# A layernorm, attention and spiking-FFN kernel: blocks 6 and 7 scaled by GpSimd and transposed by VectorE, and a lead of ten steps for the score maxima

## The chip, the cores and the metric

The kernel runs on one core of a Trainium2 chip. The metric is the device time of one launch, in microseconds (us); 3 runs of the kernel before gave a median of 1691.6 us (1691.52 to 1691.74). A core has TensorE (PE, matmuls), VectorE (DVE), ScalarE (ACT), GpSimd (POOL), and SyncE (SP), which here only issues DMAs. Each engine works through its own instructions in order, and they wait for one another by semaphores. Matmul results land in PSUM, which GpSimd does not touch in this kernel.

## The reference, cut to what matters

```python
xn = layernorm(x)                                  # x: 2 x 2048 x 256, float32, no affine part
q, k, v = split(xn @ w_qkv)                        # 16 heads of 16
q, k = irfft(rfft(q) * mask), irfft(rfft(k) * mask)   # mask = sigmoid(mask_logits), per head dim
attn = softmax(q @ k.T / sqrt(16)) @ v             # over 2048 keys, 2 batches x 16 heads
h = square(relu(xn @ W_fc.T)); y = h @ W_proj.T    # 1024 hidden
mem = 0                                            # then five times:
mem = 0.9 * mem + y - (mem > 1);  spk = mem > 1
out = x + attn @ w_out + b_out + mean(spk)
```

## The kernel before, in words

**The prologue** (0 to 111.5 us of the profiled execution) takes the 4096 tokens in eight blocks of 512 (`t` = 0 to 7). A block is normalised on VectorE: `block_stats` (four `bn_stats` and `bn_aggr`), `block_rstd` (a chain of small operations with one square root on ScalarE), and `block_scale` (four `tensor_scalar` of 128x256, subtract and multiply, with the mean and the reciprocal deviation as scalars per partition). The result has to be turned, because TensorE contracts over partitions. Two ways exist. Blocks in `TURNED` (1 to 5) are transposed in 32x32 squares by VectorE (`turn_block`, one instruction of 128x1024), and sixteen pieces of 32x256 are then moved to their place in `xnT`: ScalarE moves 8 (`MOVES` = 0, 2, 3, 3 behind the four `take_high` of the block before), GpSimd 8. Blocks 0, 6 and 7 are turned by eight 128x128 transposes on TensorE into PSUM (line 616), and ScalarE copies them out (`take_transposed`, line 506).

For each block TensorE then computes q and k (`project_qk`, line 659, four pieces `w` of 128x512) and v (`project_v`, line 672, eight matmuls of 128x256). The float32 matmuls are recorded as two instructions each. ScalarE rounds a piece of q or k to its high part (`take_high`, line 526), VectorE subtracts for the low part (`low_part`, line 1046), and both go to DRAM and come back as the operands `qst` and `kst` of the scores, with high and low parts stacked.

**The maxima.** Softmax needs the row maxima of the scores before the scores are made, because the shift by the maximum is added inside TensorE (line 724). So the scores are computed twice: first for the maxima, then transposed for the exponentials. A head's 2048x2048 scores have 32 units of maxima (128 queries x 1024 keys each) and 32 steps of scores. In the main loop the maxima run `LEAD` = 8 steps ahead. The first 24 units of the first head lie in the prologue: `FIRST_MAX` = 48 matmuls of 128x512 (`first_max`, TensorE line 645, VectorE line 1012), one behind every matmul of blocks 5, 6 and 7. Two halves of a PSUM buffer `mx` alternate, so that the first_max n+2 on TensorE waits until VectorE has reduced n.

**The main loop** (112.8 to 1658 us) has 16 pairs of steps for each of 32 heads (`pair`): in a pair TensorE makes four maxima matmuls (line 711), scores and shifts for two steps (lines 718 and 724), the products with V for two earlier steps (line 735), and a share of the FFN (lines 841 and 846). ScalarE takes the exponentials (line 562) and copies half a unit for VectorE (line 568); VectorE reduces the maxima (lines 1017 to 1036); GpSimd squares and runs the five spiking steps. Twice in a head `split_shift` turns 8 maxima per partition into the shift rows (VectorE lines 1058 to 1073), and SP stores them with eight DMAs (line 329). TensorE waits for these at steps 0 and 16 (`shift_in`). From step `ALONE` (8 steps into the last head) on there are no maxima left, and the pairs are shorter. The end (line 928) projects the attention output and VectorE adds the rest.

The order of every engine is written out by hand. Around the change it is set on VectorE by the loop over `t` and `w` after `normalise(1)`: in block 4 the three stages of block 6 stand behind the pieces `w` = 0, 1, 2, and the whole of block 7 behind piece 3. ScalarE waits in the same place with `deviation(7)`, and behind it stand a table load, `take_v(4)` and the first `take_high` of block 5:

```python
for w in range(QB):
    if t > 4:
        for n in range(2):
            first_max(TB * (t - 5) + 2 * w + n)
    low_part(t, w)
    if t == 4 and w < 3:
        (block_stats, block_rstd, block_scale)[w](6)
if t == 4:
    normalise(7)
```

Of the kernel before, what the change touches and what calls it, by code (L numbers as in the profile page):

```python
# [34 lines left out]
LEAD = 8  # L35
# [8 lines left out]
TURNED = range(1, 6)  # L44
MOVES = (0, 2, 3, 3)
POOL_MOVES = 16 - sum(MOVES)
USES = 3
# [22 lines left out]
def build(nc, x, wqk, wv, wout, bout, logits, wfc, wproj, dft, eye, out):  # L70
    with ExitStack() as ctx:
# [131 lines left out]
        ln_done = sem("ln_done")  # L203
        tr_done = sem("tr_done")
# [203 lines left out]
        def _(pool):  # L408
# [19 lines left out]

            pool.wait_ge(preset, PRESETS)
            for t in TURNED:  # L430
                pool.wait_ge(turned, t)
                for n, (dst, src) in enumerate(list(moves(t))[16 - POOL_MOVES:]):
                    if t > 1 or n:
                        pool.wait_ge(moved_pool, POOL_MOVES * (t - 1) + n)
                    pool.tensor_copy(dst, src).then_inc(moved_pool, 1)
            pool.wait_ge(moved_pool, POOL_MOVES * len(TURNED))

# [173 lines left out]
        def _(pe):  # L611
# [23 lines left out]
            def first_max(n):  # L635

                (tile, chunk), c = first_part(n), n % 2
                pe.wait_ge(mx_taken, n + 1)
                if n < 2:
                    pe.wait_ge(lo_done, QB * 4 + QK_BANKS + n + 1 + QK_BANKS)  # L640
                if n in (0, TB):
                    pe.wait_ge(keys_in[0][n // TB], KEYS)
                if n in (0, 2 * TB):
                    pe.wait_ge(queries_in[0][n // (2 * TB)], QUERIES)
                pe.matmul(mx[:, c, :], qst[0][:, tile * P:(tile + 1) * P], kst[0][:, chunk * BLK:(chunk + 1) * BLK],  # L645
                          start=True, stop=True).then_inc(mx_ready, 1)
# [289 lines left out]
        def _(dve):  # L936
            LN_LINKS = 7

            def block_stats(t):

                base, p = LN_LINKS * t, t % 2
# [8 lines left out]
                dve.wait_ge(ln_step, base + 1)  # L950
                dve.memset(carrier[:, 0:1], 0.0)
# [6 lines left out]
            def block_rstd(t):  # L958
                base = LN_LINKS * t
# [9 lines left out]
                dve.tensor_tensor(rstd[:, 4, :], rstd[:, 3, :], rstd[:, 2, :], ALU.mult).then_inc(ln_step, 1)  # L969
# [39 lines left out]
            def first_max(n):  # L1009
                tile, chunk = first_part(n)  # L1010
                dve.wait_ge(mx_ready, n + 1)
                dve.tensor_reduce(pmax[:, tile, chunk:chunk + 1], mx[:, n % 2, :], AX, ALU.max).then_inc(mx_taken, 1)
# [69 lines left out]
            for t in range(NB):  # L1082
# [4 lines left out]
                for w in range(QB):  # L1087
                    if t > 4:
                        for n in range(2):
                            first_max(TB * (t - 5) + 2 * w + n)  # L1090
                    low_part(t, w)
                    if t == 4 and w < 3:
                        (block_stats, block_rstd, block_scale)[w](6)
                if t < 4:
                    normalise(t + 2)
                if t == 4:
                    normalise(7)
# [42 lines left out]
            halve(1, pmax[:, TB // 2:TB, 0:2], FIRST_MAX)  # L1140
# [5 lines left out]
            def beside_maxima(h, b, s, last):  # L1146
# [6 lines left out]
                if s == LEAD + 2:  # L1153
                    for link in range(4):
                        split_shift(link, 2 * i + 1, 1, FIRST_MAX + g - 2)
# [8 lines left out]
                if s == LEAD + TB + 2 and not last:  # L1164
                    for link in range(4):
                        split_shift(link, 2 * i + 2, 0, FIRST_MAX + g - 2)
# [7 lines left out]
            def head(h, b, last=False):  # L1174
                for s in range(FIRST, STEPS + FIRST, 2):
# [11 lines left out]
                    if last and s == LEAD + TB:  # L1187
                        for t in END_LATE:
                            end_bias_of(t)
                    if last and LEAD + TB < s <= LEAD + TB + 12:  # L1190
                        end_base_of((s - LEAD - TB) // 2 - 1)
# [67 lines left out]
```

## Time and profile before

| | |
|---|---|
| median of 3 runs | 1691.6 us (1691.52 to 1691.74) |
| the profiled execution itself | 1691.07 us |
| its span, first to last instruction | 1689.3 us |
| busy: PE / DVE / ACT / POOL | 1681.4 / 1494.2 / 1330.1 / 719.7 us |
| granted TensorE clock | 1.0 of full speed |

Busy time alone does not show which engine is the bottleneck. What the end depends on is read from the chain of waits, which follows the last instruction back through whatever released each step. Idle times in square brackets in a timeline stand for the time just before a row and its releaser. The profiled execution is 1.8 us longer than its span.

### The profile page before, as it was taken

The numbers are of one execution on the slowest core, as the hardware profiler recorded it, in microseconds if no ns is written. First come the engines' busy times: TensorE is split into PE (matmuls) and PEld (weight loads), VectorE is DVE, ScalarE is ACT, GpSimd is POOL, SyncE is SP. The second block draws the span as 40 slices with busy tenths as digits, with TensorE's granted clock in tenths as the row PEclk, the third lists the DMA queues.
The fourth block names the chain that finished last, engine by engine and source line by source line (L and its number), as shares of the span: only waits on it lengthen the run. The fifth ranks groups of instructions, "written<-read, shape, count | busy, mean of one in ns | idle before, by whom it ended". The sixth has DMA issues, their size and how long they took to land.

```text
span 1689.3 us, 44435 instructions
## 1 busy us (share of the span) xinstructions
PE 1681.4 (100%) x17842; PEld 1145.9 (68%) x17842; DVE 1494.2 (88%) x2375; ACT 1330.1 (79%) x1718; POOL 719.7 (43%) x979
## 2 busy tenths in 40 slices
PE   9999999999999999999999999999999999999999
PEld 6566666666666666666666666666666666666667
DVE  6889999998999999989998999999989998999884
ACT  5548888888888888888888888888888888888872
POOL 3103334555433345554333455543335554333455
PEclk9999999999999999999999999999999999999999
DMA  6851122112211221122112211221122112211133
GB/s 216 294 161 47 33 54 55 51 33 55 55 50 34 55 55 43 41 55 55 43 41 55 56 37 47 55 55 36 48 55 56 31 53 55 55 30 54 43 105 103
DMA packets 95406, 108.02 MB, mean 64 GB/s; under 512 B 56032, under 2 KB 70240, under 8 KB 95200
## 3 DMA queue, kind: packets, MB, share of 16 engines
q1 hardware_dynamic: 91744, 101.97, 21.2%
q10 hardware_dynamic: 3456, 3.21, 0.6%
q8 instruction: 141, 2.31, 0.6%
q14 instruction: 65, 0.53, 0.1%
HBM read 78.91 MB, written 20.97 MB: 59 GB/s over the span
## 4 chain that ended last, share of the span: by engine, by line
PE 98%; DVE 1%; ACT 0%; issue 0%; ACTq 0%; POOL 0%; POOLq 0%
PE banks L735 31%; PE ring L711 22%; PE ring L718 14%; PE ring L724 14%; PE banks L841 7%; PE banks L846 3%; PE banks L659 2%; PE ring L928 2%; PE ring L672 1%; PE ring L645 1%; PE ring L659 1%; PE ring L686 0%; DVE stats L947 0%; DVE attnT L979 0%; ACT xnT L513 0%
## 5 line engine op out<-in xcount | busy, mean ns | idle before, releaser
L562 ACT ACTIVATE probs<-ring 128x1024 f32<-128x1024 f32 x1024 | 1002.1, 1026 | 6.5 <-PE ring L724 6.2
L711 PE MATMUL ring<-kst,qst 64*128 64x512 f32 x2000 | 674.7, 417 | 0.3 <-ACT probs L562 0.3
L735 PE MATMUL banks<-probs,vst 128*32 128x256 f32 x8192 | 548.2, 385 | 0.1
L1036 DVE TENSOR_REDUCE pmax<-ring 128x2 f32<-128x1024 f32 x407 | 497.7, 1223 | 12.7 <-PE ring L711 0.5
L568 ACT ACTIVATE half_sb<-ring 128x512 f32<-128x512 f32 x500 | 299.2, 598 | 261.4 <-PE ring L711 254.1
L718 PE MATMUL ring<-qst,kst 64*128 64x512 f32 x2048 | 493.0, 425 | 0.1
L711 PEld LDWEIGHTS ring<-kst,qst 64*128 64x128 f32 x2000 | 328.3, 184 | 208.3 <-issue 204.6
L1017 DVE TENSOR_REDUCE pmax<-ring 128x1 f32<-128x512 f32 x500 | 345.4, 691 | 88.7 <-PE ring L711 85.1
L724 PE MATMUL ring<-shift_rows,ones 64*128 64x512 f32 x2048 | 422.9, 390 | 0.0
L1023 DVE TENSOR_REDUCE pmax<-half_sb 128x1 f32<-128x512 f32 x500 | 335.5, 671 | 37.0 <-ACT half_sb L568 33.1
L735 PEld LDWEIGHTS banks<-probs,vst 128*32 128x32 f32 x8192 | 213.7, 109 | 209.7 <-issue 91.0
L841 PE MATMUL banks<-xnT,wfc_sb 64*128 64x128 f32 x2024 | 331.7, 284 | 0.1
L464 POOL TENSOR_TENSOR lif<-lif 128x256 f32<-128x256 f32 x32 | 19.7, 614 | 729.6 <-ACT y_sb L586 729.6
L846 PE MATMUL banks<-wproj_sb,hid_sb 64*128 64x256 f32 x1024 | 329.0, 401 | 0.0
L841 PEld LDWEIGHTS banks<-xnT,wfc_sb 64*128 64x128 f32 x2024 | 280.6, 186 | 19.6 <-PE ring L711 0.4
L718 PEld LDWEIGHTS ring<-qst,kst 64*128 64x128 f32 x2048 | 233.4, 185 | 26.5 <-ACT probs L562 3.6
L724 PEld LDWEIGHTS ring<-shift_rows,ones 64*128 64x128 f32 x2048 | 214.8, 185 | 17.2
L846 PEld LDWEIGHTS banks<-wproj_sb,hid_sb 64*128 64x128 f32 x1024 | 169.6, 184 | 10.9
L474 POOL TENSOR_SCALAR lif<-lif 128x256 f32<-128x256 f32 x128 | 110.1, 860 | 10.8
L475 POOL TENSOR_SCALAR lif<-lif 128x256 f32<-128x256 f32 x128 | 110.6, 864 | 8.0
L473 POOL TENSOR_TENSOR lif<-lif 128x256 f32<-128x256 f32 x128 | 95.1, 743 | 10.0
L471 POOL TENSOR_TENSOR lif<-lif 128x256 f32<-128x256 f32 x128 | 94.3, 737 | 10.0
(96 smaller groups left out, 1050.9 us busy)
## 6 DMA issues: line engine op xcount, KB each, us to landing
kst<-qk_scratch SPq DMA_DIRECT2D x256, 128.0 KB, 3.0
qst<-qk_scratch SPq DMA_DIRECT2D x256, 128.0 KB, 2.9
qk_scratch<-attnT SPq DMA_DIRECT2D x32, 256.0 KB, 3.0
shift_rows<-shiftT SPq DMA_DIRECT2D x512, 2.0 KB
qk_scratch<-probs SPq DMA_DIRECT2D x16, 256.0 KB, 3.0
attnT<-o_turned SPq DMA_DIRECT2D x256, 16.0 KB, 1.9
xnT<-x SPq DMA_DIRECT2D x8, 512.0 KB, 5.6
out<-xnT SPq DMA_DIRECT2D x7, 512.0 KB, 2.9
```

Of the source, the lines that this page charges most:

```text
L475: pool.tensor_scalar(decayed, mem, BETA, None, ALU.mult).then_inc(lif_step, 1)
L562: act.activation(probs[:, s % PS, :], score_slot(g), ACT.Exp, scale=SCALE).then_inc(exp_done, 1)
L568: act.activation(half_sb[:], unit_slot(2 * p)[:, BLK:2 * BLK], ACT.Copy).then_inc(half_taken, 1)
L711: return pe.matmul(unit_slot(g)[:, c * BLK:(c + 1) * BLK], qst[b][rows, tile * P:(tile + 1) * P], kst[b][rows, key:key + BLK], start=True, ...
L718: pe.matmul(score_slot(g)[:, c * BLK:(c + 1) * BLK], kst[b][rows_of(side), kt * P:(kt + 1) * P], qst[b][rows_of(side), q:q + BLK], start=T ...
L724: mm = pe.matmul(score_slot(g)[:, c * BLK:(c + 1) * BLK], ones[rows_of(side), :], shift_rows[rows_of(side), q:q + BLK], start=False, stop= ...
L735: mm = pe.matmul(po[32 * j:32 * (j + 1), half * D:(half + 1) * D], vst[b][:, kt, :], quarters[:, j], start=(kt == 0), stop=(kt == TB - 1))
L841: return pe.matmul(misc[:, (f % 4) * P:(f % 4 + 1) * P], wfc_sb[rows_of(side), c, f * P:(f + 1) * P], xnT[rows_of(side), c, tile * P:(tile ...
L846: return pe.matmul(misc[:, 0:D], hid_sb[rows_of(side), f, :], wproj_sb[rows_of(side), f, :], start=(f == 0 and side == 1), stop=(f == FC - ...
L1017: dve.tensor_reduce(pmax[:, tile, 2 * part:2 * part + 1], unit_slot(g)[:, 0:BLK], AX, ALU.max).then_inc(mx_taken, 1)
L1023: dve.tensor_reduce(pmax[:, tile, 2 * part + 1:2 * part + 2], half_sb[:], AX, ALU.max).then_inc(half_max, 1)
L1036: dve.tensor_reduce(pmax[:, tile, 2 * part:2 * part + 2], unit_slot(g).rearrange("p (c e) -> p c e", c=2), AX, ALU.max).then_inc(mx_taken, 1)
```

## The change

Three things change. GpSimd scales blocks 6 and 7 (`scale_block`), behind its moves of blocks 5 and 6; VectorE transposes them like blocks 1 to 5 (`TURNED` = 1 to 7), block 6 between the low parts of block 4 and the statistics of block 7, and block 7 inside block 5. GpSimd moves ten of the sixteen pieces and ScalarE six. And `LEAD` is 10: the first 44 instead of 48 first_max stay in the prologue, and the maxima in the last head go on for one pair more. The positions of `split_shift` in a head (steps 10 and 26) stay; `turn_output` goes from steps 12 and 28 to 14 and 30. In the code:

```diff
-LEAD = 8
+LEAD = 10
-TURNED = range(1, 6)
-MOVES = (0, 2, 3, 3)
+TURNED = range(1, 8)
+MOVES = (0, 2, 2, 2)
 POOL_MOVES = 16 - sum(MOVES)
+AFTER_MOVES = {6: 5, 7: 6}
...
+            def scale_block(t):
+                p = t % 2
+                pool.wait_ge(rstd_ready, t - NB + 3)
+                pool.wait_ge(turned, t - 2)
+                pool.wait_ge(moved_pool, POOL_MOVES * AFTER_MOVES[t])
+                for k in range(KT):
+                    last = pool.tensor_scalar(x_norm[:, p, k, :], x_in[:, p, k, :], meanvar[:, k, 0:1],
+                                              rstd[:, 4, k:k + 1], ALU.subtract, ALU.mult)
+                last.then_inc(ln_done, 1)
...
+                for n in (NB - 2, NB - 1):
+                    if AFTER_MOVES[n] == t:
+                        scale_block(n)
...
             def first_max(n):
+                if n >= FIRST_MAX:
+                    return
...
                 dve.wait_ge(ln_step, base + 1)
+                if t == NB - 1:
+                    dve.wait_ge(ln_done, NB - 1)
...
-                dve.tensor_tensor(rstd[:, 4, :], rstd[:, 3, :], rstd[:, 2, :], ALU.mult).then_inc(ln_step, 1)
+                last = dve.tensor_tensor(rstd[:, 4, :], rstd[:, 3, :], rstd[:, 2, :], ALU.mult)
+                last.then_inc(rstd_ready if t >= NB - 2 else ln_step, 1)
...
-                    if t == 4 and w < 3:
-                        (block_stats, block_rstd, block_scale)[w](6)
+                    if t == 4 and w < 2:
+                        (block_stats, block_rstd)[w](6)
+                    if t == 5 and w == 2:
+                        turn_block(7)
...
                 if t == 4:
-                    normalise(7)
+                    turn_block(6)
+                    block_stats(7)
+                    block_rstd(7)
...
-                if s == LEAD + 2:
+                if s == LEAD:
                     for link in range(4):
-                        split_shift(link, 2 * i + 1, 1, FIRST_MAX + g - 2)
+                        split_shift(link, 2 * i + 1, 1, FIRST_MAX + g)
...
-                if s == LEAD + TB + 2 and not last:
+                if s == LEAD + TB and not last:
                     for link in range(4):
-                        split_shift(link, 2 * i + 2, 0, FIRST_MAX + g - 2)
+                        split_shift(link, 2 * i + 2, 0, FIRST_MAX + g)
```

Where the instructions go, on VectorE first, from the last low parts of block 4 (`relu_sb`, `hid_sb`) to the third piece of block 5 in the kernel before. `probs<-attnT` would be a `turn_block`; `attnT<-attnT,meanvar,rstd` is a `block_scale`; `pmax<-ring` are first_max:

```order
L1046 TENSOR_TENSOR relu_sb<-ring,relu_sb 128x512
L979 TENSOR_SCALAR attnT<-attnT,meanvar,rstd 128x256 x4
L1046 TENSOR_TENSOR hid_sb<-ring,hid_sb 128x512
L947 BN_STATS stats<-attnT 128x6 x4
...
L969 TENSOR_TENSOR rstd<-rstd 128x4
L979 TENSOR_SCALAR attnT<-attnT,meanvar,rstd 128x256 x4
L1012 TENSOR_REDUCE pmax<-ring 128x1 x2
L1046 TENSOR_TENSOR attnT<-banks,attnT 128x512
```

The same place on VectorE now, as far as the transpose of block 7:

```order
L1072 TENSOR_TENSOR relu_sb<-ring,relu_sb 128x512
L1072 TENSOR_TENSOR hid_sb<-ring,hid_sb 128x512
L1013 STREAM_TRANSPOSE probs<-attnT 128x1024
L968 BN_STATS stats<-attnT 128x6 x4
...
L992 TENSOR_TENSOR rstd<-rstd 128x4
L1038 TENSOR_REDUCE pmax<-ring 128x1 x2
...
L1072 TENSOR_TENSOR attnT<-banks,attnT 128x512
L1013 STREAM_TRANSPOSE probs<-attnT 128x1024
L1038 TENSOR_REDUCE pmax<-ring 128x1 x2
```

Both `block_scale` are gone, and two transposes have come; the first stands ahead of the statistics of block 7. GpSimd before, from the last memset of the start to the first instructions of the main loop (`ISA` is the configuration instruction that the trace calls MODIFY_POOL_CONFIG):

```order
L419 MEMSET shift_rows 128x2048
L435 COPY xnT<-probs 32x4x2x32 x40
L440 COPY vst<-v_all 128x16x16
L452 ISA
L452 TENSOR_TENSOR hid_sb<-relu_sb 128x512
```

GpSimd now, the same stretch:

```order
L421 MEMSET shift_rows 128x2048
L447 COPY xnT<-probs 32x4x2x32 x50
L437 ISA
L437 TENSOR_SCALAR attnT<-attnT,meanvar,rstd 128x256 x4
L447 COPY xnT<-probs 32x4x2x32 x10
L437 TENSOR_SCALAR attnT<-attnT,meanvar,rstd 128x256 x4
L447 COPY xnT<-probs 32x4x2x32 x10
L455 COPY vst<-v_all 128x16x16
L467 TENSOR_TENSOR hid_sb<-relu_sb 128x512
```

The configuration instruction now stands between the moves of block 5 and the first scaling; the second scaling stands behind the ten moves of block 6.

## Rows read from the trace of the kernel before

**Rows 1.** The page's chain that ended last, shares by engine.
```profile
PE 98%; DVE 1%; ACT 0%; issue 0%; ACTq 0%; POOL 0%; POOLq 0%
```

**Rows 2.** Chain of waits, block 4: start us, length us, what.
```profile
51.45 0.69 DVE attnT L1046
...
56.77 1.25 DVE probs L989
...
64.71 1.31 DVE stats L947 x4
...
67.93 1.38 DVE attnT L979 x4
```

**Rows 3.** Timelines, blocks 0 to 5: start us, us, engine, line, operation [idle before].
```profile
22.95 3.70 PE L659 MATMUL banks<-xnT,counts 128*128 128x512 f32 x8 [0.31 <-ACT xnT L513]
...
58.08 3.63 POOL L435 COPY xnT<-probs 32x256 f32<-32x256 f32 x8 [6.48 <-DVE probs L989]
...
64.03 0.69 DVE L1046 TENSOR_TENSOR hid_sb<-ring,hid_sb 128x512 fp32r<-128x512 f32 x1
...
66.91 1.28 ACT L556 ACT_TABLE_LOAD   x1
...
68.31 1.01 ACT L530 ACTIVATE v_all<-ring 128x1024 f32<-128x1024 f32 x1
...
69.21 0.59 ACT L526 ACTIVATE attnT<-banks 128x512 fp32r<-128x512 f32 x1
69.23 1.28 DVE L1012 TENSOR_REDUCE pmax<-ring 128x1 f32<-128x512 f32 x2
69.97 0.50 PE L645 MATMUL ring<-kst,qst 128*128 128x512 f32 x1 [1.44 <-DVE pmax L1012]
...
74.99 0.68 DVE L1012 TENSOR_REDUCE pmax<-ring 128x1 f32<-128x512 f32 x1
```

**Rows 4.** Chain of waits, blocks 5 to 7.
```profile
75.94 0.87 PE ring L616 x8
...
77.25 0.23 PE ring L645
...
82.10 0.86 PE banks L659 x2
...
97.02 0.86 PE banks L659 x2
...
111.53 1.34 PE banks L898 x12
```

**Rows 5.** GpSimd: timeline rows; one of the view of line 452.
```profile
112.84 0.40 POOL L440 COPY vst<-v_all 128x256 f32<-128x256 f32 x1 [51.14 <-issue]
115.75 1.04 POOL L452 TENSOR_TENSOR hid_sb<-relu_sb 128x512 f32<-128x512 f32 x1 [2.52 <-ACT relu_sb L573]
...
152.77 0.87 POOL L465 TENSOR_SCALAR lif<-y_sb 128x256 f32<-128x256 f32 x1
153.70 0.86 POOL L466 TENSOR_SCALAR lif<-y_sb 128x256 f32<-128x256 f32 x1
...
L452 POOLq MODIFY_POOL_CONFIG  x2: 3/3/3, 113.2 to 113.2; - x2
```

**Rows 6.** Last head: chain, SP's timeline, and DMA issues with us to landing.
```profile
1623.77 1.01 PE banks L735 x16
...
1626.80 1.01 PE banks L735 x16
...
1629.38 1.01 PE banks L735 x16
...
1637.29 1.01 PE banks L735 x16
...
1628.98 5.27 SPq L329 DMA_DIRECT2D shift_rows<-shiftT  x8
...
attnT<-o_turned SPq DMA_DIRECT2D x256, 16.0 KB, 1.9
```

More of the change, by code:

```diff
@@ L203, in build @@
         ln_done = sem("ln_done")
+        rstd_ready = sem("rstd_ready")
         tr_done = sem("tr_done")
@@ L937, in _, with links @@
             LN_LINKS = 7
+            def links(t):
+                return LN_LINKS * t - (t == NB - 1)
             def block_stats(t):
-                base, p = LN_LINKS * t, t % 2
+                base, p = links(t), t % 2
                 if t:
@@ L958, in block_rstd @@
             def block_rstd(t):
-                base = LN_LINKS * t
+                base = links(t)
                 dve.wait_ge(std_ready, t + 1)
@@ L1009, in first_max @@
             def first_max(n):
+                if n >= FIRST_MAX:
+                    return
                 tile, chunk = first_part(n)
@@ L1138, in end_base_of @@
                                          in1=ends[t], op0=ALU.mult, op1=ALU.add).then_inc(end_base, 1)
-            halve(1, pmax[:, TB // 2:TB, 0:2], FIRST_MAX)
+            halve(1, pmax[:, TB // 2:FIRST_MAX // 2 - TB // 2, 0:2], FIRST_MAX)
             for s in range(0, FIRST, 2):
@@ L1186, in head @@
                             end_bias_of(t)
-                    if last and s == LEAD + TB:
+                    if last and s == TB + 8:
                         for t in END_LATE:
                             end_bias_of(t)
-                    if last and LEAD + TB < s <= LEAD + TB + 12:
-                        end_base_of((s - LEAD - TB) // 2 - 1)
+                    if last and TB + 8 < s <= TB + 20:
+                        end_base_of((s - TB - 8) // 2 - 1)
             for h in range(H - 1):
```

## The prediction

> **What bounds the kernel now.** I read the chain of waits first. It gives TensorE 98% of the span [rows 1], so an edit is worth what it takes from or adds to TensorE's row of work, and nothing else. In the main loop the chain never leaves TensorE. The change therefore acts in two places: the prologue, where the chain does leave it, and the last head, where the lead decides how many pairs carry maxima.
>
> The chain of block 4 shows the exception. From 51.45 us to the end of the scaling of block 7 at 69.31 every piece is VectorE's, apart from 0.2 us pieces of ScalarE [rows 2], while TensorE has its next blocks' columns ready. The timeline says what it costs: TensorE's third first_max at 69.97 stood behind 1.44 us of idle time released by VectorE's reduction [rows 3]. From there on the chain is TensorE's again: block 5 runs to 82.10, block 6 to 97.02, block 7 to 111.53 [rows 4]. So the question for the prologue is one: when does VectorE reach its first first_max (69.23 before), and does it keep up after that.
>
> **The change part by part.** All sums are against the profiled execution (1691.07 us, span 1689.3), whose time is 0.53 us under the median of 1691.6; I add that at the end.
>
> *ScalarE's moves.* TensorE waited 0.31 us for ScalarE's last moves of block 1 at 22.95 [rows 3]. With six moves instead of eight they end about 0.4 us earlier, and ten moves of GpSimd (at 3.63/8 = 0.454 us) end before that. TensorE is then free of waits up to block 4, and VectorE's chain starts from its results: everything comes 0.3 us sooner. **-0.3**, and it is carried in the times below.
>
> *GpSimd scales block 6.* Its moves of block 5 started at 58.08 behind VectorE's transpose [rows 3], now 57.8; ten take 4.54, to 62.35. Then four `tensor_scalar` of 128x256 with two operations and scalars per partition, which this trace does not show on GpSimd. The nearest rows are its `tensor_scalar` of 128x256 with one operation, 0.87 and 0.86 us and 0.93 from start to start [rows 5]; four of them make 3.65. The lower bound is its copy of 128x256, 0.40 us [rows 5], 1.75 for four with the gaps; the upper is twice the 0.86, 6.8. I take 1.0 each, 4.0 together, close to the one-operation row with something for the second operation. Scaling ends at 66.35, and VectorE's transpose of block 6 starts at 66.4. VectorE itself is free for it at about 64.0: its last low part of block 4 ended at 64.72 [rows 3], and now has neither a scaling in front nor a third move in front of the `take_high` that it waits for. So VectorE stands idle for 2.4 us, and what is queued behind the waiting transpose is all of block 7's statistics and then the first_max, for which TensorE waits.
>
> *VectorE up to the first first_max.* Transpose 1.25 (as at 56.77), then statistics to reciprocal deviation, 64.71 to 67.93 = 3.22 [rows 2]; the scaling of block 7 is gone. 66.4 + 1.25 + 3.22 = 70.9, against 69.23: 1.6 us later, although 2.8 us of scaling left VectorE.
>
> *What is late next.* ScalarE stood in `deviation(7)` as well. Behind it come a table load of 1.28, `take_v(4)` of 1.01 and the first `take_high` of block 5, which began at 69.21, that is 4.50 after the statistics began at 64.71 [rows 2, 3]. Before, VectorE's scaling covered that. Now it begins at 67.65 + 4.5 = 72.15 and ends at 72.75, while VectorE is through two first_max (1.28 us [rows 3]) at 72.15. VectorE idles 0.6 us for the low part.
>
> *VectorE inside block 5.* From 72.75 it has four low parts, fourteen first_max and the transpose of block 7. Reductions follow each other at 0.60 (two take 1.28, one 0.68 [rows 3]); I count low parts the same. 18 x 0.60 + 1.25 = 12.05, so 84.8. TensorE may leave block 5 about one reduction earlier, at 84.2. Its own columns need less: 82.10 - 69.97 = 12.1 before, minus the eight transposes, 0.87 [rows 4]. VectorE is the bound through all of block 5, and the transposes' 0.87 is not seen. Block 6 starts at 84.2 against 82.10: **+2.1**. Is block 7 scaled in time? GpSimd: transposed 67.65, ten moves 4.54, scaling 4.0, makes 76.2; VectorE gets there after seven pieces of 0.60 from 72.75, at 76.95. Only 0.75 us of cover.
>
> *Block 6 and 7.* Block 6 took 14.92 us with transposes, block 7 14.51 without [rows 4], although a bare eight transposes are 0.87: without them TensorE waits for a low part. So **-0.4** for block 6. In block 7 four first_max of 0.23 each [rows 4] go: **-0.9**. VectorE has slack there (20 x 0.60 = 12.0). The main loop starts 2.1 - 0.4 - 0.9 = 0.8 later.
>
> *The main loop.* `split_shift` keeps its steps, and `turn_output` moves by one pair. SP's loads of the next queries and keys stand behind it and start 3 us later, but what needs them (steps 10, 18, 26 of the maxima) moved by 3 us too. **0**, hidden by that.
>
> *The last head.* One pair more with maxima. A pair with them took 1626.80 - 1623.77 = 3.03, the first without 1629.38 - 1626.80 = 2.58 [rows 6]: **+0.45**. And a wait is added. The last shift follows the last maxima, so SP's eight stores of it start at 1628.98 + 3.03 = 1632.0, take 5.27, and with a landing of 1.9 (the row of the other small store, as an estimate; the shift stores have none) are there at 1639.2 [rows 6]. TensorE comes to step 16 at 1637.29 + 1.01 + 0.45 = 1638.75, and does nothing until they land: **+0.4**, bounds 0 and 0.9. VectorE's bias additions and the residual loads come 3 us later, in front of seven idle microseconds before the last projection.
>
> Sum: 2.1 - 0.4 - 0.9 + 0.45 + 0.4 = +1.65 (the -0.3 lies in the 2.1), so 1692.7, and at the level of the median **1693.3 us**, +0.1%. What a measurement here can tell from no change is 0.2%, 3.4 us.
>
> **Two rules of the Trainium skill.** The one-input instruction of GpSimd in this trace is 0.40 as a copy and 0.86 as a `tensor_scalar`, both 128x256 [rows 5]. The Trainium skill, "GPSIMD Engine Reference", section 4.1 (Engine selection), calls one-input work roughly line-rate; by that rule the scaling would cost like the copy, the sum would be -0.6, and the trace's `tensor_scalar` does not agree. By the row it is +1.65.
>
> The configuration instruction that now stands in front of the first scaling ran at 113.2 and the next instruction started at 115.75, 0.08 after what it waited for; what it loads took 2.5 us at most, maybe nothing [rows 5]. I take 0. The Trainium skill, "GPSIMD Engine Reference", section 2.1 (Instruction dispatch), gives about 6 us from this instruction to the first use of freshly loaded code; by an estimate from that page's figure the sum would be about +7.6, 1699.2, and the trace does not agree for the instruction that it shows.
>
> **The rivals.**
> *The scaling is dear (slower).* One mechanism: GpSimd's stretch S of four scalings is in front of VectorE once at block 6, and a second time at block 7 once S is over 4.75 (ready at 68.2 + 2S, needed at 72.95 + S). The time is +1.65 + (S - 4.0), plus (S - 4.75) from there. It is slower by over 3.4 us when S passes 5.25, 1.31 us per instruction; at the upper bound of 6.8 it gives +6.5, 1698.1. For it: two operations where the row has one, scalars read per partition. Against it: the two one-operation rows (a comparison and a multiplication elsewhere) cost the same, as if the loop did not depend on the operation.
> *The configuration load is exposed.* 0 to 2.5 us in front of block 6, added once: up to +4.1, 1695.7. For it: before, this instruction stood in a pause of GpSimd and could hide anything up to that. Against it: the next instruction started 0.08 after its release. That the load takes longer in the new place than the 2.5 us it had in the old one is a small rest of this case.
> *The scaling costs like a copy.* GpSimd ends at 64.1, with VectorE: all 2.25 us of that come back, -0.6, 1691.0. For it only the copy's row.
> *The main loop is disturbed.* If later loads or `turn_output` cost 0.1 us in each of 32 heads, +3.2 and 1696.5. Against it: the chain shows no wait there.
> *Faster by over 0.2%.* It would take all of the 1.44 wait, both sets of transposes and the four first_max at once, 1.44 + 1.74 + 0.9, with nothing paid in the last head. The rows of VectorE exclude it nearly.
>
> **How the numbers follow.** Forecast (S between 3.6 and 4.6, no load) 0.50; dear scaling 0.20; exposed configuration up to 2.5 us 0.13, longer 0.04; like a copy 0.09; main loop 0.04. Over 3.4 us slower are most of the dear case, half of the exposed, and the last ones: 0.30. Faster by over 0.2%: 0.04. The rest 0.66. The range leaves out the far end of the dear case, the longer configuration and the lowest edge of the copy case: 1691.0 to 1697.2.
>
> **What would show it.** GpSimd's four scalings near 4.0 us with VectorE's transpose of block 6 directly behind them, at about 66.4; first_max 0 near 70.9; the first low part of block 5 behind a `take_high` near 72.2; block 6 from 84.2 without a pause on VectorE in block 5; 0.4 to 0.5 us of wait ahead of v in blocks 5 and 6; in the last head a pair of 3.03 in place of 2.58 and a TensorE wait of under 1 us at step 16. I am wrong if VectorE does not wait for GpSimd at block 6, if the configuration instruction is followed by a gap, or if pairs of the main loop are longer than before.

## The result, and the profile after

The changed kernel takes **1696.64 us** (median of 7 runs, 1696.16 to 1697.27) against 1691.52 of the kernel before (7 runs on the same chip, 1690.85 to 1691.80). The ratio is 1.0032, 95% interval 1.0023 to 1.0042: slower by 0.3%, 5.1 us. The forecast was 1693.3, +1.65 us, with "no change that can be told" as its likeliest case. The sign was right and the time lies inside the range; the size was 3.5 us too small. The prediction called up to 3.4 us no change (chance 0.66) and gave a slowdown beyond that 0.30; the 5.1 us are such a slowdown.

The profiled execution took 1696.16 us, span 1693.8. The page's busy times and its chain by engine, to be read against [rows 1]:

```profile
PE 1681.3 (99%) x17826; PEld 1147.5 (68%) x17826; DVE 1504.8 (89%) x2368; ACT 1329.7 (79%) x1719; POOL 739.0 (44%) x1017
...
PE 97%; DVE 1%; POOL 0%; issue 0%; DMA 0%; ACT 0%; ACTq 0%; SPq 0%; POOLq 0%
```

TensorE is still the bound, and the one per cent that it lost says nothing of where. So I cut the span at the starts of the blocks and of the last head's pairs. The chain of waits, to be read against [rows 4] and [rows 6] (start us, length us, what):

```profile
63.67 3.64 POOL attnT L437 x3
...
72.68 0.80 PE ring L662
73.48 1.71 PE banks L676 x2
75.18 0.43 PE ring L662
...
86.56 0.86 PE banks L676 x2
...
101.08 0.86 PE banks L676 x2
...
114.65 1.34 PE banks L915 x12
...
1630.83 1.02 PE banks L752 x16
1633.87 1.02 PE banks L752 x16
1636.70 1.00 PE banks L752 x16
```

GpSimd's scaling now stands in the chain. Block 6 starts at 86.56 (82.10 before), block 7 at 101.08, the work behind the blocks at 114.65 (111.53 before). The pair that runs from 1630.83 to 1633.87 takes 3.04 where a pair without maxima took 2.58. The difference of the two profiled executions then splits like this:

| piece | forecast | measured | from |
|---|---|---|---|
| start of block 6 | +2.1 | +4.46 | 86.56 - 82.10 |
| block 6 | -0.4 | -0.40 | 14.52 against 14.92 |
| block 7 | -0.9 | -0.94 | 13.57 against 14.51 |
| one pair more with maxima | +0.45 | +0.46 | 3.04 against 2.58 |
| wait for the last shift | +0.4 | 0 | below |
| rest of the main loop | 0 | +0.94 | 1544.22 against 1542.82, less 0.46 |
| outside the span | - | +0.6 | 2.36 against 1.77 |
| sum | +1.65 | +5.1 | |

Three entries ask for a cause: the 2.4 us by which block 6 is later than forecast, the 0.94 of the main loop, and the 0.6 outside the span (the measured time less the span).

The timelines of GpSimd, VectorE, ScalarE and TensorE at block 6 (start us, busy us, engine, line, operation, idle time before it and what ended it), against [rows 3]:

```profile
57.66 4.56 POOL L447 COPY xnT<-probs 32x256 f32<-32x256 f32 x10 [5.70 <-DVE probs L1013]
62.44 4.86 POOL L437 TENSOR_SCALAR attnT<-attnT,meanvar,rstd 128x256 f32<-128x256 f32 x4 [0.22 <-POOL xnT L447]
67.33 1.25 DVE L1013 STREAM_TRANSPOSE probs<-attnT 128x1024 f32<-128x1024 f32 x1 [3.45 <-POOL attnT L437]
68.64 4.58 POOL L447 COPY xnT<-probs 32x256 f32<-32x256 f32 x10 [1.34 <-DVE probs L1013]
70.75 1.28 ACT L571 ACT_TABLE_LOAD   x1
71.94 1.28 DVE L1038 TENSOR_REDUCE pmax<-ring 128x1 f32<-128x512 f32 x2
72.68 0.80 PE L662 MATMUL ring<-kst,qst 128*128 128x512 f32 x1 [5.30 <-DVE pmax L1038]
73.42 4.83 POOL L437 TENSOR_SCALAR attnT<-attnT,meanvar,rstd 128x256 f32<-128x256 f32 x4 [0.20 <-POOL xnT L447]
73.67 0.69 DVE L1072 TENSOR_TENSOR attnT<-banks,attnT 128x512 fp32r<-128x512 f32 x1 [0.45 <-ACT attnT L541]
75.65 0.69 DVE L1038 TENSOR_REDUCE pmax<-ring 128x1 f32<-128x512 f32 x1 [0.68 <-PE ring L662]
77.89 0.69 DVE L1038 TENSOR_REDUCE pmax<-ring 128x1 f32<-128x512 f32 x1 [0.36 <-PE ring L662]
79.10 1.24 DVE L1013 STREAM_TRANSPOSE probs<-attnT 128x1024 f32<-128x1024 f32 x1
80.96 0.50 PE L662 MATMUL ring<-kst,qst 128*128 128x512 f32 x1 [0.50 <-DVE pmax L1038]
```

The foretold order is there: ten moves, four scalings, VectorE's transpose directly behind them after 3.45 us of waiting, the statistics, the first reduction, and TensorE behind that. The configuration instruction ran at 62.23 and the scaling started at 62.44, so it costs 0.2 us at most; the idle time before the second scaling, which has no such instruction in front, is 0.20 too against 0.22, so hardly any of it is the instruction's. The second transpose, at 79.10, did not wait: block 7 was scaled in time.

Two things are not as foretold. The scalings take 4.86 us instead of 4.0. And from 74.9 to 77.9 VectorE waits for TensorE (0.68, 0.36), where I had VectorE as the bound in all of block 5; only later, from the transpose of block 7 on, does TensorE wait for VectorE again (0.50 at 80.96). The table by stretches shows why. Its columns are the stretch and its length, the busy time and count of TensorE, its weight loads, VectorE, ScalarE and GpSimd, then the granted clock, the DMA share and GB/s:

```profile
71.00:72.00 1.00, 0.00 (x0) 0.00 (x0) 0.90 (x5) 1.00 (x1) 0.88 (x3) 1.00 0.67 217
72.00:73.00 1.00, 0.32 (x1) 0.32 (x2) 1.00 (x3) 0.99 (x3) 0.88 (x3) 0.61 0.24 78
73.00:74.00 1.00, 1.00 (x2) 0.51 (x2) 0.55 (x2) 0.64 (x2) 0.80 (x2) 0.50 0.00 0
74.00:75.00 1.00, 1.00 (x3) 0.36 (x2) 0.96 (x2) 0.00 (x0) 1.00 (x2) 0.50 0.00 0
75.00:76.00 1.00, 1.00 (x5) 0.67 (x3) 0.35 (x1) 0.78 (x2) 1.00 (x2) 0.69 0.76 283
76.00:77.00 1.00, 1.00 (x4) 0.52 (x3) 1.00 (x3) 0.53 (x2) 1.00 (x1) 1.00 0.65 242
```

TensorE had been idle for 5.30 us in one piece; then its granted clock was 0.50, which is 1.2 of 2.4 GHz, until about 75.6. The matmul of a first maximum took 0.80 there where [rows 3] show 0.50, and two matmuls of the columns 1.71 where 0.86 is usual. Before, after 1.44 us of idle time [rows 3], the same table reads:

```profile
69.00:72.00 3.00, 2.03 (x7) 1.22 (x7) 3.00 (x6) 1.40 (x3) 0.00 (x0) 1.00 0.70 191
72.00:75.00 3.00, 3.00 (x9) 1.54 (x9) 2.71 (x6) 0.60 (x1) 0.00 (x0) 1.00 0.91 346
```

SP's row for the last shift, against [rows 6]:

```profile
1636.17 5.26 SPq L331 DMA_DIRECT2D shift_rows<-shiftT  x8
```

The issue of its eight stores ends at 1641.43. TensorE's next group of products with V began at 1641.81, 2.55 us behind the one before (1639.26), the wait for the shift stands behind it, at 1642.8, and the following group began at 1644.38: no wait.

### The profile page after: what moved, and what is told of

The parts are those of the page before. It is cut to its first block, busy times and chain, and to the rows that moved or that the text cites. A ratio compares the mean times of both kernels' runs of the same rounds, so it can differ in the third digit from the quotient of the medians.

```text
span 1693.8 us, 44439 instructions
## 1 busy us (share of the span) xinstructions
PE 1681.3 (99%) x17826; PEld 1147.5 (68%) x17826; DVE 1504.8 (89%) x2368; ACT 1329.7 (79%) x1719; POOL 739.0 (44%) x1017
## 4 chain that ended last, share of the span: by engine, by line
PE 97%; DVE 1%; POOL 0%; issue 0%; DMA 0%; ACT 0%; ACTq 0%; SPq 0%; POOLq 0%
PE banks L752 30%; PE ring L728 22%; PE ring L735 14%; PE ring L741 14%; PE banks L858 7%; PE banks L863 4%; PE banks L676 2%; PE ring L945 2%; PE ring L689 1%; PE ring L676 1%; PE ring L662 1%; DVE pmax L1038 0%; POOL xnT L447 0%; DMA attnT<-x 0%; POOL attnT L437 0%
## 5 line engine op out<-in xcount | busy, mean ns | idle before, releaser
L479 POOL TENSOR_TENSOR lif<-lif 128x256 f32<-128x256 f32 x32 | 20.2, 632 | 731.0 <-ACT y_sb L601 731.0
L467 POOL TENSOR_TENSOR hid_sb<-relu_sb 128x512 f32<-128x512 f32 x64 | 66.6, 1041 | 76.9 <-ACT relu_sb L588 76.9
L486 POOL TENSOR_TENSOR lif<-lif 128x256 f32<-128x256 f32 x128 | 95.2, 744 | 10.0
```

## The experiments

The theory: GpSimd's scaling, 0.86 us longer than I took it, makes TensorE's idle time 5.3 us long, and this idle time costs a second time through the clock. The rivals: VectorE's own row of work is the whole loss, whoever scales; the longer lead costs time in the main loop; the extra is no more than the variation between executions. The kernels ran in three groups, each beside the kernel before: e1 to e4 (its median 1691.67 of 29 runs), e5 to e8 (1691.94 of 33), the repeats and e9 (1691.78 of 15). "To block 6" is the time from VectorE's first reduction of a first maximum to the start of block 6 in the chain; "prologue" runs from the first columns of block 5 to the start of the work behind the blocks; "span" is the median of the spans of all timed executions.

| kernel | median us | span | ratio [95%] | idle TensorE | to block 6 | prologue |
|---|---|---|---|---|---|---|
| before, medians of the three groups, three profiles | 1691.67, 1691.94, 1691.78 | 1689.8, 1690.1, 1690.0 | - | 1.44, 1.45, 1.44 | 12.87, 12.86, 12.84 | 46.31, 46.28, 46.28 |
| after, two profiles | 1696.64 | 1694.0 | 1.0032 [1.0023, 1.0042] | 5.30, 5.30 | 14.62, 15.78 | 50.57, 51.67 |
| e1 | 1694.45 | 1692.5 | 1.0016 [1.0007, 1.0025] | 3.81 | 14.85 | 49.32 |
| e2 | 1696.50 | 1694.7 | 1.0028 [1.0018, 1.0039] | 5.25 | 16.14 | 52.95 |
| e3 | 1690.59 | 1688.3 | 0.9992 [0.9983, 1.0001] | 0.78 and 0.73 | 13.46 | 45.49 |
| e4 | 1693.95 | 1692.1 | 1.0014 [1.0005, 1.0023] | 0.51 | 13.80 | 49.71 |
| e5 | 1694.11 | 1692.0 | 1.0014 [1.0005, 1.0023] | 4.04 | 15.55 | 50.26 |
| e6 | 1691.27 | 1689.5 | 0.9997 [0.9988, 1.0006] | 1.44 | 12.83 | 45.31 |
| e7 | 1689.66 | 1687.6 | 0.9988 [0.9979, 0.9997] | 0.77 and 0.21 | 13.14 | 44.84 |
| e8 | 1692.75 | 1691.0 | 1.0004 [0.9995, 1.0013] | 0.36 | 13.20 | 47.66 |
| e9 | 1689.70 | 1687.7 | 0.9987 [0.9978, 0.9996] | 0.80 and 0.20 | 13.13 | 45.73 |

Median and span have to be read together. In the kernel before the time outside the span was 1.75 to 1.92 us in all 77 executions beside the experiments, in the changed kernel 1.97 to 2.87 with a median of 2.5. So 0.7 of the 5.1 us lie outside the span, and no piece of work in the prologue explains them. The clock's fall is not enough to bring them: e2, whose clock falls like that of the changed kernel, has 1.76 to 1.86, and e3, whose clock does not fall, 1.78 to 2.97. What it is stays open. What an experiment does to the prologue is therefore given by spans too below.

**e1, VectorE scales.** Only who scales is undone; transposes on VectorE, ten moves and lead stay.

```diff
-                for n in (NB - 2, NB - 1):
-                    if AFTER_MOVES[n] == t:
-                        scale_block(n)
...
-                    if t == 4 and w < 2:
-                        (block_stats, block_rstd)[w](6)
+                    if t == 4 and w < 3:
+                        (block_stats, block_rstd, block_scale)[w](6)
...
                     block_rstd(7)
+                    block_scale(7)
```

> The changed kernel, but VectorE scales blocks 6 and 7 again (GpSimd only moves; VectorE still transposes both). Theory A, the wait for GpSimd and what follows from it: VectorE starts the transpose of block 6 at about 64.4 instead of 67.33, comes to the first first_max at 64.4 + 1.25 + 3.22 + 1.4 = 70.3 instead of 71.94, and has no wait for a take_high; block 6 of the projections starts at about 83 instead of 86.56. Time 1693.0 to 1694.3, the upper end if TensorE's clock still falls in its idle time. Theory B, the transposes on VectorE inside block 5 are what costs, not GpSimd: within 0.5 of the changed kernel's 1696.6.

VectorE's transpose stands at 63.88 instead of 67.33, but the scaling of block 7 is back in front of the reductions, which start at 70.12. TensorE is idle for 3.81 us and loses its clock all the same. Timeline row of TensorE and two stretches:

```profile
70.85 0.80 PE L659 MATMUL ring<-kst,qst 128*128 128x512 f32 x1 [3.81 <-DVE pmax L1033]
...
70.00:71.00 1.00, 0.15 (x1) 0.15 (x1) 1.00 (x3) 0.17 (x1) 0.00 (x0) 0.94 0.63 205
71.00:72.00 1.00, 1.00 (x2) 0.69 (x3) 1.00 (x3) 0.00 (x0) 0.00 (x0) 0.50 0.50 148
```

GpSimd's scaling costs 1696.64 - 1694.45 = 2.2 us in the medians. In the spans it is 1.5, and the idle time of TensorE is 1.49 shorter (5.30 to 3.81). So the wait for GpSimd is real, but it is the smaller part: 2.8 us of loss remain without it, more than I had expected (block 6 starts at 84.97, not at 83, and the median is 0.15 above my range). The transpose of block 6 in VectorE's row ahead of the first maxima is enough to keep TensorE idle until its clock falls; e8 parts what the clock takes of the 2.8 us from the rest.

**e2, a lead of eight.** The changed kernel with `LEAD = 8` and the shift where it was.

> The changed kernel with the lead of 8 steps of the kernel before (48 first_max in the prologue, turn_output at steps 12 and 28), only the block 6 and 7 part of the change left. Theory A: the prologue 0.9 us longer, the last head 0.46 shorter, 1697.1. Rival C: the main loop of the changed kernel is 0.9 us longer than that of the kernel before by the lead or turn_output, and gets it back here: 1695.7 to 1696.2.

Block 7 took 14.53 us against 13.57, which is the four first maxima of the shorter lead. The medians do not move, 1696.50 and 1696.64, between what the two theories had said (1697.1, and 1695.7 to 1696.2); the span is 0.7 us longer, where 0.9 less 0.46 was expected. In its profile the granted clock stayed low from 72.1 to 78.9, 6.8 us, against 3.4 in the first profile of the changed kernel.

**e3, statistics of their own.** Two sets of mean and deviation take away what makes block 7's statistics wait for block 6's scaling, and the transposes of blocks 6 and 7 go behind the first two reductions of blocks 5 and 6.

```diff
+        meanvar_of = [sb(f"meanvar{i}", [P, KT, 2]) for i in range(2)]
+        rstd_of = [sb(f"rstd{i}", [P, 5, KT]) for i in range(2)]
...
-                if t == NB - 1:
-                    dve.wait_ge(ln_done, NB - 1)
...
+                    if t > 4 and t < 7 and w == 0:
+                        turn_block(t + 1)
                     low_part(t, w)
...
-                    if t == 5 and w == 2:
-                        turn_block(7)
...
-                    turn_block(6)
                     block_stats(7)
```

> The changed kernel with two sets of mean and deviation buffers, so that VectorE computes block 7's statistics while GpSimd scales block 6; the transposes of blocks 6 and 7 stand behind the first two first_max of blocks 5 and 6. Theory A: first first_max near 67, no idle time of TensorE over 1 us, projections of block 6 from about 80.3, main loop 3.3 us earlier than in the kernel before and 6.4 earlier than in the changed one. Time 1688.3 to 1690.3, faster than both. Rival C, the lead of ten or the later turn_output costs in the main loop: 1691 or more, with pairs of the main loop longer by 0.9 us in the sum.

Timeline rows of VectorE and TensorE, and the chain's row at which the work behind the blocks starts:

```profile
66.98 1.28 DVE L1041 TENSOR_REDUCE pmax<-ring 128x1 f32<-128x512 f32 x2
68.18 1.24 DVE L1016 STREAM_TRANSPOSE probs<-attnT 128x1024 f32<-128x1024 f32 x1
...
67.72 0.50 PE L664 MATMUL ring<-kst,qst 128*128 128x512 f32 x1 [0.78 <-DVE pmax L1041]
70.05 1.13 PE L678 MATMUL banks<-xnT,counts 128*128 128x512 f32 x2 [0.73 <-DVE attnT L1075]
...
109.13 1.34 PE banks L917 x12
```

GpSimd scales as slowly as in the changed kernel (4.84 us), yet the first reduction is at 66.98 instead of 71.94, TensorE's idle time is 0.78, and the loss is gone: 6.05 us less than the changed kernel (1696.64 to 1690.59). It is 1.1 us under the kernel before of its group, which its interval cannot tell from nothing. So with the same slow scaling the kernel is no slower than before when VectorE does not stand behind it: what is dear is the place of the wait and of the transpose, at the head of VectorE's row, in front of statistics that only share a buffer. The run moves both at once and does not part them. The prologue ended at 109.13, about 1 us later than I expected, and the time is 0.3 above my range: TensorE waited a second time (0.73), and block 6 took 15.1 us with the transpose of block 7 in one piece at its start.

**e4, TensorE kept at work.** Eleven matmuls whose result nothing reads stand in front of the wait for the first reduction; nothing else changes.

```diff
+                if n == 2:
+                    for _ in range(FILL):
+                        pe.matmul(even_slot[:, 0:D], lif[:, 4, 0:P], lif[:, 4, :], start=True, stop=True)
                 pe.wait_ge(mx_taken, n + 1)
```

> The changed kernel with eleven matmuls of zeros (128x256, results unused) on TensorE directly ahead of its wait for the first reduction, 4.7 us of its 5.3 us idle time. Theory A: the granted clock stays at 1.0 after 72.7 instead of 0.5, the two pieces of 128x512 behind it take 0.86 instead of 1.71 and 0.93, VectorE's waits for TensorE at 75.65 and 77.89 go, and the time falls by 1.0 to 1.5 us, to about 1695.4. Rival: block 5 is bound by VectorE, the slow clock lies beside its work, and nothing moves by more than 0.3.

TensorE's timeline and two stretches:

```profile
66.69 4.91 PE L658 MATMUL ring<-lif 128*128 128x256 f32 x22
72.11 0.50 PE L666 MATMUL ring<-kst,qst 128*128 128x512 f32 x1 [0.51 <-DVE pmax L1042]
...
72.00:73.00 1.00, 0.89 (x4) 0.61 (x4) 0.65 (x2) 1.00 (x2) 0.74 (x3) 1.00 0.00 0
73.00:74.00 1.00, 0.83 (x4) 0.20 (x3) 0.88 (x2) 0.58 (x3) 1.00 (x1) 1.00 0.00 0
```

Useless work of 4.91 us (22 records of the eleven) makes the kernel 2.7 us faster in the median and 1.9 in the span: the wait for VectorE stays (its first reduction comes 7.82 us behind the first columns of block 5, 7.86 in the changed kernel), the clock stays at 1.00, the first maximum's matmul takes 0.50 again. This is the experiment that shows the clock's share, 1.9 us; the other 0.7 are the time outside the span. The 1.9 are more than the 1.0 to 1.5 that I had expected, because I went by the first profile of the changed kernel, which has one of its short slow stretches.

**e5, one operation.** The scaling leaves out the subtraction of the mean: one multiplication by a scalar per partition.

```diff
-                    last = pool.tensor_scalar(x_norm[:, p, k, :], x_in[:, p, k, :], meanvar[:, k, 0:1],
-                                              rstd[:, 4, k:k + 1], ALU.subtract, ALU.mult)
+                    last = pool.tensor_scalar(x_norm[:, p, k, :], x_in[:, p, k, :], rstd[:, 4, k:k + 1],
+                                              None, ALU.mult)
```

> The changed kernel, but GpSimd's eight scalings of 128x256 multiply only, by the same scalar per partition; the subtraction of the mean is left out. They took 1.22 us each with both operations. Theory A1, the second operation is what costs: 0.86 like the one-operation rows of the kernel before, the four 3.65 instead of 4.86, TensorE's idle time 1.2 us shorter and the time lower by 1.2 to 2, near 1695. Rival A2, the scalars read per partition cost: 1.22 each and no change of the time.

The view of the scaling's line, of the changed kernel and then of e5 (min/median/max ns, first and last start):

```profile
L437 POOL TENSOR_SCALAR attnT<-attnT,meanvar,rstd x8: 1220/1222/1233, 62.4 to 77.0; 128x256 f32<-128x256 f32 x8
```

```profile
L437 POOL TENSOR_SCALAR attnT<-attnT,rstd x8: 920/922/926, 61.9 to 74.3; 128x256 f32<-128x256 f32 x8
...
70.92 0.80 PE L662 MATMUL ring<-kst,qst 128*128 128x512 f32 x1 [4.04 <-DVE pmax L1038]
```

The second operation, together with its own scalar per partition, costs 0.30 us, the first scalar per partition 0.06 (0.92 against 0.86 [rows 5], where the scalar is a constant). That is 1.2 us less in front of VectorE's transpose, and TensorE idles 1.26 us less. The median fell by 2.5 us (I had allowed 2) and the span by 2.0, both more than the 1.2; what the other 0.8 of the span are, this run does not show. The length of the slow stretch differs from execution to execution (6.8 us in this profile) and may be part of it.

**e6, the lead alone.** The kernel before with `LEAD = 10` and all that hangs on it, nothing else.

> The kernel before with the lead of ten steps alone (44 first_max in the prologue, turn_output at steps 14 and 30). Theory A: prologue 0.93 shorter, last head 0.46 longer, so 0.5 us faster than before, which this measurement cannot tell from nothing: 1690.5 to 1691.7. Rival C, the lead costs in the main loop: pairs longer by 0.5 to 1 us in the sum, 1692 or more.

1691.27 against 1691.94, ratio 0.9997 [0.9988, 1.0006]. The prologue is 1.0 us shorter, as forecast (0.93) for the four first maxima; in the total nothing can be told.

**e7, transposes in halves.** e3, with each of the two transposes in two pieces of 128x512 ahead of two low parts, and the table load moved behind the first high part of block 5.

```diff
+                    if t in (5, 6) and w < 2:
+                        turn_half(t + 1, w)
                     low_part(t, w)
...
+                    if t == 5 and w == 0:
+                        act.activation(filt[:, 1:2], filt[:, 0:1], ACT.Exp)
```

> The version with two sets of statistics, and the transposes of blocks 6 and 7 made in two halves of 128x512 behind the first_max of pieces 0 and 1, and ScalarE's table load behind the first take_high of block 5. If the waits of 0.73 us at 70.05 and the 0.6 us that block 6 ran too long were the transposes in one piece and the table load: block 6 from 79.5, main loop from 107.9 instead of 109.1, time about 1689.3, clear of the kernel before by over 2 us. If VectorE is simply full there: within 0.4 of 1690.6.

The two waits of TensorE are now 0.77 and 0.21, and block 6 takes 14.8 us:

```profile
68.25 0.50 PE L665 MATMUL ring<-kst,qst 128*128 128x512 f32 x1 [0.77 <-DVE pmax L1052]
70.04 1.12 PE L679 MATMUL banks<-xnT,counts 128*128 128x512 f32 x2 [0.21 <-DVE attnT L1086]
...
109.02 1.34 PE banks L918 x12
```

1689.66 us, 0.9988 [0.9979, 0.9997]: 7.0 us under the changed kernel and 2.3 under the kernel before. The interval excludes one, the size is within the 0.2% that I call no change. Transposes and table load were moved together, so the run does not say which of them gave the 0.9 us against e3. Block 6 started at 80.65 and the blocks ended at 109.02, both 1.1 us later than I had expected. VectorE is busy for 13.00 of the 13.14 us from its first reduction (67.51) to the start of block 6, so its row is full there, as the rival said, and shorter waits elsewhere cannot make block 5 much shorter.

**e8, VectorE scales and TensorE is kept at work.** e1 with eight of e4's matmuls.

> VectorE scales, as in the first experiment, and eight matmuls of zeros fill 3.4 of TensorE's 3.8 us idle time. If the wait for GpSimd and TensorE's clock are two separate parts of the loss, both gains add: 1.5 us or more under the 1694.45 without the fill, near 1692.7. If the clock does not matter there: 1694.3.

1692.75 against e1's 1694.45 is 1.7 us through the clock (2.0 against each one's own kernel before, 1.5 in the spans), and the way to block 6 fell by 1.65, from 14.85 to 13.20. What is left of the loss is 0.8 us, ratio 1.0004 [0.9995, 1.0013]. So without GpSimd's scaling and without the clock's fall the change stands at the level of the kernel before. The rival of VectorE's own row is wrong as the whole loss; but without GpSimd's scaling that row still left TensorE idle for 3.81 us, and this brought the clock down.

**Both kernels once more.** The kernel before twice and the changed one once, for their variation.

> The kernel before once more, for a second profile of its main loop. From the start of the FFN matmuls (line 898) to the last group of products with V it took 1542.82 us in the first profile. The kernels with a lead of ten took 1543.60 to 1544.52 in eight profiles, of which 0.46 is the pair more with maxima. If the 0.3 to 1.2 us beyond that are variation from execution to execution, this one lies anywhere from 1542.8 to 1544.0; if they come from the lead, it is again within 0.2 of 1542.8.

> The same as the run before it, a third profile of the kernel before: 1542.8 to 1544.0 if the main loop varies by itself, within 0.2 of 1542.8 if the lead of ten makes it longer.

> The changed kernel once more. Its first profile had TensorE at half clock from 72.7 to about 75.6 and projections of block 6 from 86.56; the same stretch of the kernel with the lead of eight was at half clock to about 78.5 and came to block 6 at 88.31. If the length of the slow stretch varies from execution to execution while the wait for GpSimd does not, VectorE waits 3.4 to 3.5 us for GpSimd again, and block 6 starts anywhere from 86.4 to 88.4, moved by the length of the slow stretch.

From the first columns of block 5 to the end of the blocks the kernel before took 46.31, 46.28 and 46.28 us, the changed one 50.57 and 51.67. Before does not vary there, after does. The stretches of the second profile of the changed kernel:

```profile
70.00:71.00 1.00, 0.00 (x0) 0.00 (x0) 0.66 (x4) 0.83 (x2) 0.83 (x3) 0.90 0.57 184
71.00:72.00 1.00, 0.00 (x0) 0.00 (x0) 0.93 (x4) 0.99 (x3) 0.86 (x3) 0.50 0.53 189
...
77.00:78.00 1.00, 1.00 (x4) 0.58 (x3) 0.59 (x1) 0.00 (x0) 0.88 (x1) 0.69 0.58 219
```

Same idle time (5.30), VectorE behind GpSimd as long as before, but the clock fell while TensorE was still idle and was back only at about 77.6; block 6 started at 87.35. The main loop, from the start of the work behind the blocks to the last group of sixteen products with V, was 1542.82, 1544.21, 1544.26 in the three profiles of before and 1543.50, 1543.55 in the two of e2 and e9, which have a lead of eight too: mean 1543.67. Nine profiles with a lead of ten have a mean of 1544.11. The difference is 0.44, near the 0.46 of the pair with maxima. The five profiles with a lead of eight spread over 1.4 us, so this excludes neither a few tenths for the lead nor none. But the 0.94 lies within what one and the same kernel does, and nothing is left that would need the rival of the main loop. (The two repeats of the kernel before lie 0.2 to 0.3 above the 1544.0 that I had as their upper end.)

**e9, e7 with a lead of eight.**

> The version with own statistics and transposes in halves, with the lead of eight. If the lead of ten is worth what its two rows say (0.93 less, 0.46 more), this is 0.5 us slower than 1689.66, 1690.1; if ten steps cost in the main loop what the profiles had beyond that, it is 0.3 or more faster.

1689.70 against 1689.66, between the two forecasts (0.5 slower, 0.3 or more faster). The prologue is 0.89 longer (45.73 against 44.84), the last head's pair comes back. The lead is worth under 0.5 us in the rows (0.9 less 0.46), and no total shows it.

## Why the prediction was right and wrong

**Right in mechanism.** That VectorE would wait for GpSimd at block 6 and TensorE for VectorE, in front of block 5, with blocks 6 and 7 giving back 0.4 and 0.9 and a pair of the last head taking 0.46: each has its row above. The configuration instruction, taken at 0, cost 0.2 at most, and block 7 was scaled in time. The Trainium skill, "GPSIMD Engine Reference", section 2.1 (Instruction dispatch), gives about 6 us from this instruction to the first use of freshly loaded code. This trace has nothing like it (62.23 to 62.44), and no run shows whether any code was loaded here.

**Mis-sized: the scaling.** The term "1.0 each, 4.0 together" measured 1.22 and 4.86. I took the row of one operation as the neighbour and put too little on top for the second: e5 shows 0.30 for it. This makes the transpose 67.33 instead of 66.4 and the first reduction 71.94 instead of 70.9, 1.0 us. The 4.86 lie outside the forecast case (S between 3.6 and 4.6) and in the rival "dear scaling", chance 0.20; but by that rival's own formula they give 1.65 + 0.86 + 0.11 = +2.6, 1694.2, and its second half, a wait for block 7, did not occur. So this alone is about half of the measured 5.1.

**Missing: the clock.** The step "VectorE is the bound through all of block 5" failed: from 72.7 to 77.9 TensorE was the bound, at half clock until 75.6, and VectorE waited for it. The step priced the matmuls of block 5 by rows at full clock, although the same working made TensorE idle for about 3 us (1.44 and 1.6 more), a length that no row of the kernel before had, and it became 5.30. From the first reduction to block 6 I had 84.2 - 70.9 = 13.3 us; e4, at full clock, took 13.80, the changed kernel 14.62 and 15.78. So 0.5 us were too little by my count of pieces, and 0.8 and 2.0 us are the clock's in these two executions. In the spans it is 1.9 us (after less e4) and 1.5 (e1 less e8). The 1.9 are more than the 0.8 of the first profile because five of the seven executions of the changed kernel had a mean granted clock of 0.998, like the second profile, and the first profile had 0.999. The Trainium skill, "TensorE: Matmul & The Clock Gate", states in its section "Why this matters for your kernels" that idle gaps between bursts bring the clock down to its lower level; here the trace agrees, at 5.3, 3.81, 4.04 and 5.25 us of idle time. I had no term for it, although a rule that speaks against a change is what one should look for.

**Wrong: the last shift.** The +0.4 rested on the landing of another store, 1.9 us, counted from the end of the last issue. That end is 1641.43; TensorE's wait for these rows stands behind the products with V that end at 1642.8, and no gap follows, so they were there within 1.4 us. Counted from the start of the last of the eight issues (5.26/8 = 0.66 us earlier, 1640.8) the 1.9 would end at 1642.7, in time. The runs do not show whether this landing is shorter or was counted from the wrong end.

**Small and unnoticed.** The first columns of block 5 started at 64.08 against 65.22. I had -0.3 for ScalarE's moves; ten profiles with six moves lie at 63.55 to 64.36, four with eight moves (before and e6) at 64.59 to 65.58, 1.2 us apart in the mean. Most of it is a second wait for ScalarE's moves, which the trace of before shows ahead of block 5 and which I had not read; it is gone in the changed kernel:

```profile
65.22 1.13 PE L659 MATMUL banks<-xnT,counts 128*128 128x512 f32 x2 [0.71 <-ACT xnT L513]
```

In the changed kernel, whose VectorE hung on GpSimd, the earlier start only makes TensorE's idle time longer: the 5.30 are the 1.44 of before, 2.7 for the later reduction (71.94 against 69.23) and 1.1 for the earlier start. In e3 and e7, where VectorE does not hang on GpSimd, this is part of the gain over the kernel before.

**The sum, corrected.** 1.65 + 1.0 (scaling) + 0.5 (pieces of block 5) - 0.4 (shift) + 1.9 (clock, spans) + 0.7 (outside the span) = 5.35, against 5.1 measured; the 0.2 between them is less than the main loop varies by. That the time lies inside the stated range, 0.6 under its upper end, is luck: the upper part was there for a dear scaling and an exposed configuration instruction, and the clock and the time outside the span filled it, for which the sum had no term. Two things stay open: what the 0.7 outside the span are, and what sets how long the slow stretch is in an execution (3.4 and 6.8 us were seen after the same idle time).

## What to carry to other kernels

When a step makes the bounding engine idle in one long piece, do not only add the idle time: look whether a row shows the engine's speed after a pause of that length, and carry a term for it if none does. A wait belongs behind the work that does not need it; a shared buffer of a few numbers (the mean and deviation here) can put half an engine's row behind a slow neighbour, and here a second copy with the transpose put behind the first reductions gave back 6.05 us in the median (5.7 in the span), more than the change had cost. And look at the time outside the span as well before a whole difference of medians is put down to the place that was edited. Filling the pause with work that nobody reads tells the clock's share from the wait's.

## What the hardware showed that I had not expected

After 3.8 to 5.3 us of idle time TensorE ran at 1.2 instead of 2.4 GHz for 3.4 us in two profiles (the changed kernel's first, e1) and 6.8 in three (its second, e2, e5), so both after the same 5.30 of idle time in one kernel; after 1.44 and 0.78 us it did not. GpSimd's `tensor_scalar` of 128x256 takes 0.86 us with one operation, 0.92 with a scalar per partition, 1.22 with two operations and two such scalars, so there the number of operations does count; VectorE takes 0.35 for the last (three of block 5's in 1.06). The main loop of one and the same program varies by 1.4 us between executions (1542.82 to 1544.26), more than any term of the sum but one (2.1), though I had worked them out to the tenth.
